# A graph layer and a routed FFN on one core: the graph weight centred over its rows, raw x transposed and multiplied, and the reciprocal deviation applied when the product is split

## The chip, the cores and the metric

The kernel runs on one core of one Trainium2 chip. The metric is the device time of one execution in microseconds (us); lower is better. Five engines work side by side and meet at semaphores: TensorE (PE in the rows, its weight loads PEld), VectorE (DVE), ScalarE (ACT), GpSimd (POOL) and SyncE (SP), which only issues transfers.

## The reference

`x` is 4096 x 256, `adj` a 4096 x 4096 matrix of zeros and ones, both in float32.

```python
deg = jnp.maximum((adj != 0).astype(jnp.float32).sum(-1), 1.0)
x = x + gnn(_layernorm(x), adj, deg[..., None], W, b)
x = x + ffn(_layernorm(x)[None], Wr, br, W1, b1, W2, b2)[0]

def _layernorm(x, axis=-1, eps=1e-05):
    m = jnp.mean(x, axis=axis, keepdims=True)
    v = jnp.var(x, axis=axis, keepdims=True)
    return (x - m) / jnp.sqrt(v + eps)

def gnn(x, adjacency, node_degree, W, b):
    a_hat = adjacency + jnp.eye(n)
    dinv = jax.lax.rsqrt(node_degree)
    pooled = (dinv * a_hat * dinv) @ x + x
    return jax.nn.relu(pooled @ W + b)
```

`ffn` sends each token to two of 16 experts (256 to 512 to 256, GELU between) and adds the weighted results to its input. The change concerns the first layernorm and its product with `W` alone.

## The kernel before, in words

The 4096 rows are 32 tiles of 128 (`T = 32`). The kernel has three stages.

**The first tile.** For each of the 32 row tiles, n = 0 to 31, the product y = layernorm(x) @ W is made and kept in two float16 parts, `yh` and `yl`, whose sum carries more digits than one of them. A tile passes through the engines like this: VectorE takes its statistics (`stats_of`, L797) and, once for a chunk of eight tiles, turns them into mean and variance (`stats`, L803 to L819); GpSimd raises the variance to the power -1/2 and makes the shift (`rstd0`, L1221 and L1224), again for eight tiles in one instruction; ScalarE writes the normalised tile (`normalize`, L703); TensorE transposes it (`x_T`, L499); ScalarE copies the transpose out of PSUM (`copy_x_T`, L710); TensorE multiplies it with W (`x_times_W`, L507); ScalarE writes the high part (`high_y`, L714); VectorE writes the low part (`low_y`, L839). ScalarE runs `normalize(n)`, `copy_x_T(n - 1)`, `high_y(n - 2)` in that order for each n, and each engine takes its instructions strictly in the order of its program.

In the same loop TensorE already works on the first tile of the graph product: at step n it adds the contribution of row tile j = n - 6 (`LAG = 6`; `neighbours`, L484 and L486), which needs `y_low(j)` and, at j = 0, 8, 16 and 24, the adjacency chunk that VectorE has turned (`transpose_chunk`, L832, counted by `at_made`). VectorE's program says where the four chunks are turned: chunk 0 after `low_y(3)`, chunks 1 to 3 at the start of the next group of eight, that is after `low_y(7)`, `low_y(15)` and `low_y(23)`.

**The other 31 tiles** of the graph product follow, 64 float16 products each, then the **expert stage** over 79 blocks of 128 tokens.

x comes in 16 transfers of 256 KB, four to a chunk of eight tiles: chunks 0 and 1 half from SP's queue and half from ACT's, chunks 2 and 3 from SP's. W is one transfer of 256 KB on SP's queue (L349). The adjacency comes from POOL's queue (L252), four transfers to a tile. Names in the rows: `wall` is the large buffer that holds x, the normalised tiles, their transposes and the two parts of y; `orows` holds W; `bank` is a PSUM bank; `abuf` the adjacency as it arrived and `at_xg` as it was turned.

Of the kernel before, what the change touches and what calls it, by code (L numbers as in the profile page):

```python
# [52 lines left out]
XR = 4  # L53
# [31 lines left out]
def build(nc, x, adj, gnn_W, gnn_b, Wr, br, W1, b1, W2, b2, out):  # L85
# [13 lines left out]
    xn = wall[:, 0:2 * XR * D].bitcast(F32).rearrange("p (n d) -> p n d", d=D)  # L99
    xnT = wall[:, 2 * XR * D:2 * (XR + 2) * D].bitcast(F32).rearrange("p (n d) -> p n d", d=D)  # L100
# [49 lines left out]
    mean = sb("mean", [P, T], F32)  # L150
    rstd = sb("rstd", [P, T], F32)
    st6 = sb("st6", [P, XC, XT, 6], F32)
    var8 = sb("var8", [P, XC, XT], F32)
    dif8 = sb("dif8", [P, XT], F32)
    minus = sb("minus", [P, T], F32)
    shift0 = sb("shift0", [P, T], F32)
# [36 lines left out]
    tri = st6.rearrange("p c k s -> p (c k s)").bitcast(F16)[:, 0:E * E].rearrange("p (e f) -> p e f", f=E)  # L193
# [9 lines left out]
    ps_Y = (banks[6], banks[7])  # L203
# [231 lines left out]
    def _(pe):  # L435
# [57 lines left out]

        def x_T(n):
            after(pe, "x_normed", n)
            if n >= 2:
                after(pe, "x_T_copied", n - 2)
            for c in range(DC):
                mm = pe.transpose(ps_xT[n % 2][:, c * P:(c + 1) * P], xn[:, n % XR, c * P:(c + 1) * P], id32[:, :])  # L499
            mm.then_inc(ev("x_T"), 1)  # L500

        def x_times_W(n):
            after(pe, "x_T_copied", n)
            if n >= 2:
                after(pe, "y_low", n - 2)
            for c in range(DC):
                mm = pe.matmul(ps_Y[n % 2][:, 0:D], xnT[:, n % 2, c * P:(c + 1) * P], wg_arrival[:, c, :],  # L507
                               start=c == 0, stop=c == DC - 1)
            mm.then_inc(ev("y_made"), 1)

        def first_tile():

            for n in range(T + LAG):
                if n < T:
                    x_T(n)
                if 0 <= n - 1 < T:
                    x_times_W(n - 1)
                j = n - LAG
                if j >= 0:
# [37 lines left out]
        pe.wait_ge(ev("constants"), CONSTANTS)  # L557
        pe.wait_ge(ev("w_gnn_in"), 16)
        pe.matmul(ps_P[:, 0:E], ones16[:, :], firsts[:, :], start=True, stop=True)
# [87 lines left out]
    def _(act):  # L647
# [50 lines left out]
        def normalize(n):  # L698
            if n % XT == 0:
                after(act, "x_shift", n // XT)  # L700
            if n >= XR:
                after(act, "x_T", n - XR)
            act.activation(xn[:, n % XR, :], xin[:, n, :], ACT.Identity, scale=rstd[:, n:n + 1], bias=shift0[:, n:n + 1])\  # L703
               .then_inc(ev("x_normed"), 1)

        def copy_x_T(n):
# [3 lines left out]
            act.activation(xnT[:, n % 2, :], ps_xT[n % 2][:, 0:D], ACT.Copy).then_inc(ev("x_T_copied"), 1)  # L710
# [9 lines left out]
        for n in range(T + 2):  # L720
            if n < T:
                normalize(n)
            if 0 <= n - 1 < T:
                copy_x_T(n - 1)
            if 0 <= n - 2 < T:
                high_y(n - 2)
            if n == 2:
# [62 lines left out]
    def _(dve):  # L790
# [3 lines left out]
        def stats_of(c, k):  # L794
            if k == 0:
                V.wait_ge(x_in[c], 16 * Q)
            V.bn_stats(st6[:, c, k, :], xin[:, c * XT + k, :]).then_inc(ev("bn"), 1)  # L797

        def stats(c):
            after(V, "bn", c * XT + XT - 1)  # L800
            m_e, m_o = st6[:, c, :, 1], st6[:, c, :, 4]
            v_e, v_o = st6[:, c, :, 2], st6[:, c, :, 5]
            V.tensor_tensor(mean[:, c * XT:(c + 1) * XT], m_e, m_o, ALU.add).then_inc(ev("mean_sum"), 1)  # L803
            V.tensor_tensor(dif8[:, :], m_e, m_o, ALU.subtract).then_inc(ev("dif"), 1)
            V.tensor_tensor(var8[:, c, :], v_e, v_o, ALU.add).then_inc(ev("var_sum"), 1)
            after(V, "mean_sum", c)
            V.tensor_scalar(minus[:, c * XT:(c + 1) * XT], mean[:, c * XT:(c + 1) * XT], -0.5, None, ALU.mult)\
             .then_inc(ev("minus_made"), 1)
            after(V, "minus_made", c)
            after(V, "dif", c)  # L810
            V.tensor_tensor(dif8[:, :], dif8[:, :], dif8[:, :], ALU.mult).then_inc(ev("dif2"), 1)

            after(V, "dif2", c)
            after(V, "var_sum", c)
            V.scalar_tensor_tensor(out=var8[:, c, :], in0=dif8[:, :], scalar=D / 4.0, in1=var8[:, c, :],
                                   op0=ALU.mult, op1=ALU.add).then_inc(ev("var_made"), 1)
            after(V, "var_made", c)

            V.tensor_scalar(var8[:, c, :], var8[:, c, :], 1.0 / D, EPS, ALU.mult, ALU.add)\  # L819
             .then_inc(ev("var_ready"), 1)  # L820

# [517 lines left out]
```

## Time and profile before

| | before |
|---|---|
| median of 3 runs | 668.12 us (667.94 to 670.16) |
| the profiled execution | 667.72 us |
| its span (first to last instruction) | 666.1 us |
| TensorE busy | 598.5 us, 90% of the span |
| VectorE busy | 456.1 us, 68% |
| GpSimd busy | 335.6 us, 50% |
| ScalarE busy | 231.9 us, 35% |
| granted TensorE clock, mean | 0.977 |

The span leaves 1.6 us of the execution outside it. A row's line numbers are those of the kernel before. The rows that the prediction uses stand in the section before it.

### The profile page before, as it was taken

The page shows a single profiled execution, that of the slowest core. Times are in us where ns is not written, and L with a number is a line of the kernel's source. Part 1 is how long each engine was busy: PE and PEld are TensorE (multiplying, and loading weights), DVE is VectorE, ACT ScalarE, POOL GpSimd, SP SyncE. Part 2 cuts the span into 40 slices and gives each one's busy share as a digit, 9 for nine tenths or more (in the row PEclk, how much of TensorE's full clock was granted, in tenths as well). Part 3 has the DMA queues.
Part 4 walks back from the last instruction along what each step waited for, and adds up shares of the span by engine and source line. Part 5 has one row for each costly group of instructions (what it writes and reads, how often), then busy time and mean ns, then how long its engine had stood idle before and what let it go on. Part 6 is the DMA issues. An engine that isn't in the chain of part 4 may idle for free. (4 is left out here: it accounts for less than half of the span.)

```text
span 666.1 us, 17021 instructions
## 1 busy us (share of the span) xinstructions
PE 598.5 (90%) x4796; PEld 462.3 (69%) x4797; DVE 456.1 (68%) x1369; ACT 231.9 (35%) x483; POOL 335.6 (50%) x375
## 2 busy tenths in 40 slices
PE   2999999999999999999943999899999999999993
PEld 1687888888888788888831666566666777676772
DVE  2665888888888788888873666577665565565562
ACT  2785333332333222333330444343433323332331
POOL 6232466667666667766451123455444444434443
PEclk9999999999999999999975999999999999999998
DMA  8908699999999989999287344566654443343420
GB/s 228 236 13 160 132 195 196 196 193 190 190 196 180 196 171 190 193 198 200 87 316 242 99 113 110 127 141 138 136 84 75 80 80 67 67 75 64 74 49 1
DMA packets 67450, 94.60 MB, mean 142 GB/s; under 512 B 9232, under 2 KB 42288, under 8 KB 66896
## 3 DMA queue, kind: packets, MB, share of 16 engines
q0 software_dynamic: 32928, 51.03, 45.4%
q1 hardware_dynamic: 32176, 40.32, 19.7%
q10 hardware_dynamic: 2304, 2.72, 1.2%
q8 instruction: 22, 0.36, 0.2%
q14 instruction: 20, 0.16, 0.1%
HBM read 103.71 MB, written 25.83 MB: 194 GB/s over the span
## 5 line engine op out<-in xcount | busy, mean ns | idle before, releaser
L484 PE MATMUL bank<-wall,at_xg 128*128 128x257 f16 x1024 | 238.6, 274 | 5.9 <-DVE at_xg L832 5.8
L486 PE MATMUL bank<-wall,at_xg 128*128 128x256 f16 x1024 | 233.1, 273 | 0.0
L1299 POOL DMA_INDIRECT out_dram<-orows,at_xg x79 | 128.1, 1622 | 179.2 <-DMA out_dram<-orows,at_xg 98.0
L590 PE MATMUL bank<-wall,feat 128*128 (+1 forms) x474 | 117.2, 384 | 10.9 <-issue 7.9
L484 PEld LDWEIGHTS bank<-wall,at_xg 128*128 128x128 f16 x1024 | 102.8, 100 | 28.0 <-DVE at_xg L832 13.9
L769 ACT ACTIVATE hgs<-hgs 128x512 f32<-128x512 f32 x79 | 49.8, 630 | 198.2 <-DVE hgs L1123 195.9
L1129 DVE SCALAR_TENSOR_TENSOR hl<-bank,xseT 128x512 f16<-128x512 f32 x79 | 54.6, 692 | 92.1 <-ACT xseT L775 68.5
L1269 POOL DMA_INDIRECT rows<-feat,posi x64 | 66.7, 1042 | 91.1 <-issue 91.1
L486 PEld LDWEIGHTS bank<-wall,at_xg 128*128 128x128 f16 x1024 | 100.3, 98 | 15.0
L613 PE MATMUL bank<-wall,xseT 128*128 (+1 forms) x632 | 108.1, 273 | 0.0
L590 PEld LDWEIGHTS bank<-wall,feat 128*128 128x128 f16 x474 | 45.9, 98 | 59.1 <-issue 23.8
L832 DVE STREAM_TRANSPOSE at_xg<-abuf 128x512 int32<-128x512 int32 x128 | 86.6, 696 | 0.4
L613 PE MATMUL bank<-wall,hl 128*128 (+1 forms) x316 | 86.1, 273 | 0.0
L252 POOL DMA_DIRECT2D abuf<-in_adj_dram x128 | 72.8, 588 | 3.7 <-DVE at_xg L832 1.5
L613 PEld LDWEIGHTS bank<-wall,xseT 128*128 128x128 f16 x632 | 61.8, 98 | 8.2
L1123 DVE SCALAR_TENSOR_TENSOR hgs<-bank,abuf 128x512 f32<-128x512 f32 x79 | 53.8, 681 | 0.1
L1112 DVE COPY feat<-bank 128x512 f16<-128x512 f16 x79 | 33.3, 422 | 23.7 <-PE bank L568 21.4
L598 PE MATMUL bank<-id,hgs 128*128 128x128 f32 x316 | 47.9, 274 | 0.0
L775 ACT ACTIVATE xseT<-bank 128x512 f16<-128x512 f32 x79 | 45.7, 578 | 0.3 <-PE bank L598 0.3
L690 ACT ACTIVATE orows<-orows,bs 128x256 f32<-128x256 f32 x32 | 19.2, 600 | 76.2 <-DVE bs L918 76.2
L568 PEld LDWEIGHTS bank<-id,at_xg 128*128 128x128 f16 x316 | 24.2, 99 | 27.1 <-issue 5.7
L1137 DVE TENSOR_SCALAR orows<-bank,at_xg 128x256 f32<-128x256 f32 x79 | 37.6, 475 | 2.3 <-PE bank L613 2.3
(146 smaller groups left out, 802.2 us busy)
## 6 DMA issues: line engine op xcount, KB each, us to landing
abuf<-in_adj_dram POOLq DMA_DIRECT2D x128, 256.0 KB
wst<-in_L_ffn_W_dram SPq DMA_DIRECT2D x32, 512.0 KB
at_xg<-rows SPq DMA_DIRECT2D x79, 136.0 KB
out_dram<-orows SPq DMA_DIRECT2D x32, 128.0 KB
abuf<-in_L_ffn_b_dram SPq DMA_DIRECT2D x4, 1024.0 KB
wall<-in_x_dram SPq DMA_DIRECT2D x12, 256.0 KB, 13.9
rows<-pad ACTq DMA_DIRECT2D x12, 136.0 KB, 2.7
out_dram<-orows,at_xg POOLq DMA_INDIRECT x79
```

The lines of the kernel that those rows point to most:

```text
L252: eng.dma_start(arrived[b * PQ:(b + 1) * PQ, k % AB, :, :], adj_v[bass.ds(pair(i, k), 1), k % 2, b, :, :, :].rearrange("n i a c -> i (n a) ...
L484: both = [lambda: pe.matmul(ps_acc[odd][:, 0:D + 1], w, yh[:, j, 0:D + 1], start=j == 0, stop=j == T - 1), lambda: pe.matmul(ps_acc[odd][: ...
L486: lambda: pe.matmul(ps_acc[odd][:, 0:D], w, yl[:, j, :], start=False, stop=False)]
L590: mm = pe.matmul(q_h[r % 2][:, :], a, w, start=n == 0, stop=n == 3 * DC - 1)
L598: mm = pe.transpose(q_g[r % 2][:, c * P:(c + 1) * P], hg[r % 2][:, c * P:(c + 1) * P], id32[:, :])
L613: mm = pe.matmul(q_o[r % 2][:, 0:D], a, w, start=False, stop=n == 3 * HC - 1)
L769: act.activation(hg[r % 2], hg[r % 2], ACT.Gelu).then_inc(ev("gelued"), 1)
L832: V.transpose(at[:, c, :].bitcast(I32).rearrange("p (n a i) -> p a n i", a=Q, i=PQ), arrived[:, k % AB, :, c * CW // CH:(c + 1) * CW // CH ...
L1123: V.scalar_tensor_tensor(out=hg[r % 2], in0=q_h[r % 2][:, :], scalar=1.0 / (SX * SW), in1=b1all[:, bass.ds(e * H, H)], op0=ALU.mult, op1=A ...
L1129: V.scalar_tensor_tensor(out=hl[:, r % 2, :], in0=q_g[r % 2][:, :], scalar=SH, in1=hh[:, r % 2, :], op0=ALU.mult, op1=ALU.subtract).then_i ...
L1269: L.indirect_dma_start(rows, at_place, feat[:, odd, k, :], None).then_inc(listed[odd], 16)
L1299: L.indirect_dma_start(out, bass.IndirectOffsetOnAxis(ap=info[r][:, 0:1].bitcast(U32), axis=0), orow[r], None, bounds_check=N - 1, oob_is_ ...
```

## The change

The mean of a row need not be taken out of x: if the mean over its rows is taken out of each column of W, a constant added to a row of x adds nothing to the product. So the change

- makes W's column means with two products against a matrix of 1/256 (`column_means`) and subtracts them from W (`centre_W`, two VectorE instructions);
- transposes x itself as it arrived; `normalize`, the means, `minus` and `shift0` are gone;
- takes the variance in nine groups of 2, 3, 3 and six times 4 tiles in place of four of 8, five VectorE instructions and one GpSimd instruction each, in place of seven and two;
- multiplies by the reciprocal deviation (with the scale of the high part in it) when the product is split: `high_y` becomes an Identity with a scale that is a column of `rstd`, and `low_y` takes the same column as its scalar;
- gives the product three PSUM banks in place of two;
- takes the statistics of tile n + 5 after `low_y(n)` (`LEAD = 5`), and turns the four adjacency chunks after `low_y(4)`, `low_y(12)`, `low_y(20)` and `low_y(28)`;
- puts W first in SP's queue, and GpSimd makes the identity matrix and the exponents before its first adjacency loads; the loads of the adjacency's second and third tile stand behind the fourth and the sixth `rstd0`.

```diff
+GROUPS = ((0, 2), (2, 5), (5, 8)) + tuple((n, n + 4) for n in range(8, 32, 4))
+LEAD = 5
...
+        sp.dma_start(wg_arrival, gnn_W.rearrange("(c p) n -> p c n", p=P)).then_inc(ev("w_gnn_in"), 16)
         for b in QUEUE[0]:
             load_x(sp, 0, b)
-        sp.dma_start(wg_arrival, gnn_W.rearrange("(c p) n -> p c n", p=P)).then_inc(ev("w_gnn_in"), 16)
...
+            for c in range(DC):
+                mm = pe.matmul(ps_mean[:, 0:D], one_dth, wg_arrival[:, c, :], start=c == 0, stop=c == DC - 1)
+            mm.then_inc(ev("w_means"), 1)
...
         def x_T(n):
-            after(pe, "x_normed", n)
+            if n % XT == 0:
+                pe.wait_ge(x_in[n // XT], 16 * Q)
...
         def x_times_W(n):
             after(pe, "x_T_copied", n)
-            if n >= 2:
-                after(pe, "y_low", n - 2)
+            if n >= 3:
+                after(pe, "y_low", n - 3)
...
         def high_y(n):
+            for g, (first, _) in enumerate(GROUPS):
+                if n == first:
+                    after(act, "rstd_made", g)
             after(act, "y_made", n)
-            act.activation(yh[:, n, 0:D], ps_Y[n % 2][:, 0:D], ACT.Copy, scale=SY).then_inc(ev("y_high"), 1)
+            act.activation(yh[:, n, 0:D], ps_Y[n % 3][:, 0:D], ACT.Identity, scale=rstd[:, n:n + 1]).then_inc(ev("y_high"), 1)
...
-        for n in range(T + 2):
+        for n in range(T + 1):
             if n < T:
-                normalize(n)
+                copy_x_T(n)
             if 0 <= n - 1 < T:
-                copy_x_T(n - 1)
-            if 0 <= n - 2 < T:
-                high_y(n - 2)
...
+                high_y(n - 1)
...
+        def variance(g):
+
+            first, end = GROUPS[g]
+            cols = slice(first, end)
+            after(V, "bn", end - 1)
+            V.tensor_tensor(dif[:, cols], st6[:, cols, 1], st6[:, cols, 4], ALU.subtract).then_inc(ev("dif"), 1)
+            V.tensor_tensor(var[:, cols], st6[:, cols, 2], st6[:, cols, 5], ALU.add).then_inc(ev("var_sum"), 1)
...
+        centre_W()
+        for n in range(LEAD):
+            stats_up_to(n)
+        for n in range(T):
+            low_y(n)
+            if n + LEAD < T:
+                stats_up_to(n + LEAD)
+            if n % XT == XT // 2:
+                transpose_chunk(0, 0, n // XT)
...
+        for g in range(len(GROUPS)):
+            rstd0(g)
+            if g in (3, 5):
+                for b in range(Q):
+                    load_adj(L, 0, (g - 1) // 2, b)
```

TensorE's program at its start, before the change. L499 is a transposition, L507 the product with W, and the brackets say what an instruction waits for.

```order
L559 MATMUL bank<-firsts,ones 128x16 [waits w_gnn_in,constants]
L499 MATMUL bank<-id,wall 128x128 [waits x_normed]
L499 MATMUL bank<-id,wall 128x128
L499 MATMUL bank<-id,wall 128x128 [waits x_normed]
L499 MATMUL bank<-id,wall 128x128
L507 MATMUL bank<-orows,wall 128x256 [waits x_T_copied]
```

And with the change, where L498 is the product for the column means, L507 the transposition and L515 the product with W.

```order
L498 MATMUL bank<-orows,wall 128x256 [waits one_dth,w_gnn_in]
L498 MATMUL bank<-orows,wall 128x256
L507 MATMUL bank<-id,wall 128x128 [waits x_in0,p_id32]
L507 MATMUL bank<-id,wall 128x128 x3
L515 MATMUL bank<-orows,wall 128x256 [waits x_T_copied,w_centred]
L515 MATMUL bank<-orows,wall 128x256
```

The transposition no longer waits for a normalised tile but for x's first chunk, and the first product waits for the centred W.

VectorE's program around the turning of the adjacency's third chunk (L832, STREAM_TRANSPOSE), before the change: it stands right behind `low_y(15)` (L839), ahead of the statistics (L797) for tiles 24 and on.

```order
L803 TENSOR_TENSOR mean<-st 128x8 [waits bn]
L804 TENSOR_TENSOR dif<-st 128x8
L805 TENSOR_TENSOR var<-st 128x8
L807 TENSOR_SCALAR minus<-mean 128x8 [waits mean_sum]
L811 TENSOR_TENSOR dif<-dif 128x8 [waits dif,minus_made]
L815 SCALAR_TENSOR_TENSOR var<-dif,var 128x8 [waits var_sum,dif2]
L819 TENSOR_SCALAR var<-var 128x8 [waits var_made]
L839 SCALAR_TENSOR_TENSOR wall<-bank,wall 128x256 [waits y_high] x4
L832 STREAM_TRANSPOSE at_xg<-abuf 128x4x4x32 [waits a_in0]
```

With the change the second chunk is turned (L838) behind `low_y(12)` (L845) and `stats_of(17)` (L808); the rows begin with the variance of group 12 to 15, which `high_y(12)` waits for.

```order
L815 TENSOR_TENSOR dif<-st 128x4 [waits bn]
L816 TENSOR_TENSOR var<-st 128x4
L818 TENSOR_TENSOR dif<-dif 128x4 [waits dif]
L820 TENSOR_SCALAR var<-var 128x4 [waits var_sum]
L824 SCALAR_TENSOR_TENSOR var<-dif,var 128x4 [waits var_eps,dif2]
L865 SCALAR_TENSOR_TENSOR gbm<-orows,gbm 64x256 [waits gb_high]
L845 SCALAR_TENSOR_TENSOR wall<-bank,rstd,wall 128x256 [waits y_high]
L808 BN_STATS st<-wall 128x6 [waits x_in2]
L845 SCALAR_TENSOR_TENSOR wall<-bank,rstd,wall 128x256 [waits y_high]
L808 BN_STATS st<-wall 128x6
L838 STREAM_TRANSPOSE at_xg<-abuf 128x4x4x32 [waits a_in0]
```

The chunk that `neighbours(8)` needs was turned behind `low_y(7)` before, and is turned behind `low_y(12)` now; the chunks for `neighbours(16)` and `neighbours(24)` move from `low_y(15)` and `low_y(23)` to `low_y(20)` and `low_y(28)`.

## Rows read from the trace of the kernel before

**Rows 1.** The page's costliest groups: busy us, mean ns, idle time before it.

```profile
L832 DVE STREAM_TRANSPOSE at_xg<-abuf 128x512 int32<-128x512 int32 x128 | 86.6, 696 | 0.4
```

**Rows 2.** Windows: stretch, its length, busy us (count) by engine, PEclk, DMA share, GB/s.

```profile
64.00:341.00 277.00, 266.73 (x2380) 225.24 (x2378) 231.12 (x880) 85.92 (x201) 176.38 (x229) 1.00 0.87 183
```

**Rows 3.** Who waited for whom in the first 80 us: total, times, longest.

```profile
ACT wall L703 <- POOL shift L1224: 11.8, 4, 8.5
PE bank L559 <- DMA orows<-in_L_gnn_W_dram: 11.8, 1, 11.8
PE bank L499 <- ACT wall L703: 3.1, 4, 1.4
```

**Rows 4.** Timeline of TensorE: start, length, what, count, idle before it.

```profile
13.29 1.18 PE L499 MATMUL bank<-id,wall 128*128 128x128 f32 x4 [1.37 <-ACT wall L703]
14.45 2.07 PE L507 MATMUL bank<-orows,wall 128*128 128x256 f32 x4
...
16.75 1.71 PE L507 MATMUL bank<-orows,wall 128*128 128x256 f32 x4
...
18.86 0.44 PE L499 MATMUL bank<-id,wall 128*128 128x128 f32 x2 [0.40 <-ACT wall L703]
...
20.31 1.03 PE L507 MATMUL bank<-orows,wall 128*128 128x256 f32 x4
...
23.55 0.27 PE L484 MATMUL bank<-wall,at_xg 128*128 128x257 f16 x1
...
26.46 0.44 PE L499 MATMUL bank<-id,wall 128*128 128x128 f32 x2 [0.92 <-ACT wall L703]
...
50.75 1.03 PE L507 MATMUL bank<-orows,wall 128*128 128x256 f32 x4
...
52.06 1.03 PE L507 MATMUL bank<-orows,wall 128*128 128x256 f32 x4
52.92 0.27 PE L484 MATMUL bank<-wall,at_xg 128*128 128x257 f16 x1
...
63.26 0.28 PE L484 MATMUL bank<-wall,at_xg 128*128 128x257 f16 x1 [1.23 <-DVE at_xg L832]
```

**Rows 5.** Timeline of ScalarE: a scaled Identity, a Copy from SBUF, one from PSUM.

```profile
17.90 0.42 ACT L729 ACTIVATE gbm<-orows 128x256 f16<-128x256 f32 x1 [0.96 <-DMA brb<-in_L_ffn_br_dram]
18.22 0.58 ACT L703 ACTIVATE wall<-wall,shift,rstd 128x256 f32<-128x256 f32 x1
...
51.82 0.38 ACT L714 ACTIVATE wall<-bank 128x256 f16<-128x256 f32 x1 [0.16 <-PE bank L507]
```

**Rows 6.** Timeline of VectorE.

```profile
6.78 2.71 DVE L797 BATCH_NORM_STATS2 st<-wall 128x6 f32<-128x256 f32 x8 [5.35 <-DMA wall<-in_x_dram]
...
16.00 0.75 DVE L797 BATCH_NORM_STATS2 st<-wall 128x6 f32<-128x256 f32 x2 [5.44 <-DMA wall<-in_x_dram]
...
52.23 0.43 DVE L839 SCALAR_TENSOR_TENSOR wall<-bank,wall 128x256 f16<-128x256 f32 x1 [0.26 <-ACT wall L714]
...
61.15 0.42 DVE L839 SCALAR_TENSOR_TENSOR wall<-bank,wall 128x256 f16<-128x256 f32 x1 [0.66 <-ACT wall L714]
...
62.50 1.29 DVE L832 STREAM_TRANSPOSE at_xg<-abuf 128x512 int32<-128x512 int32 x2
...
72.59 0.48 DVE L877 SCALAR_TENSOR_TENSOR pooled<-bank,deg,xseT 128x256 f32<-128x256 f32 x1
```

**Rows 7.** GpSimd's two powers: of 8 columns (timeline), of 1 (the tile's row: ns, min/median/max).

```profile
10.64 1.68 POOL L1221 TENSOR_TENSOR rstd<-var,mhalf 128x8 f32<-128x8 f32 x1 [1.52 <-DVE var L819]
...
L1252 POOL TENSOR_TENSOR vr<-vr,mhalf x32: 566/612/627, 66.2 to 341.3; 128x1 f32<-128x1 f32 x32
```

**Rows 8.** DMA queues (q1 SP, q10 ACT, q0 POOL) from 7 to 12 us: packets, MB.

```profile
q0 software_dynamic: 306, 0.56, 60.4%
q1 hardware_dynamic: 300, 0.37, 24.6%
q10 hardware_dynamic: 242, 0.43, 23.3%
```

More of the change, by code:

```diff
@@ L202, in build @@
     ps_xT = (banks[4], banks[1])
-    ps_Y = (banks[6], banks[7])
+    ps_Y = (banks[6], banks[7], banks[3])
+    ps_mean = banks[5]
     q_x = [b[:, :].bitcast(F16) for b in banks[0:2]]
@@ L515, in first_tile @@
                     x_T(n)
+                if n == 1:
+                    after(pe, "w_centred", 0)
                 if 0 <= n - 1 < T:
@@ L555, in step @@
                     logits(s)
[L557 to L559 removed]
+        column_means()
+        pe.wait_ge(ev("p_id32"), 2)
         first_tile()
@@ L696, in exps @@
             act.activation(ex2[:, :], p8[:, 0:1], ACT.Exp, scale=-1.0, bias=p8[:, 1:2]).then_inc(ev("exps_made"), 1)
[L698 to L704, printed above, removed]
         def copy_x_T(n):
@@ L791, in _ @@
         V = dve
[L794 to L820, printed above, removed]
@@ new lines, in centre_W, with stats_of @@
+        def centre_W():
+            after(V, "w_means", 0)
+            for c in range(DC):
+                mm = V.tensor_tensor(wg_arrival[:, c, :], wg_arrival[:, c, :], ps_mean[:, 0:D], ALU.subtract)
+            mm.then_inc(ev("w_centred"), 1)
+        def stats_of(n):
+            if n % XT == 0:
+                V.wait_ge(x_in[n // XT], 16 * Q)
+            V.bn_stats(st6[:, n, :], xin[:, n, :]).then_inc(ev("bn"), 1)
+        def variance(g):
[4 more added lines that the diff above has]
+            V.tensor_tensor(var[:, cols], st6[:, cols, 2], st6[:, cols, 5], ALU.add).then_inc(ev("var_sum"), 1)
+            after(V, "dif", g)
+            V.tensor_tensor(dif[:, cols], dif[:, cols], dif[:, cols], ALU.mult).then_inc(ev("dif2"), 1)
+            after(V, "var_sum", g)
+            V.tensor_scalar(var[:, cols], var[:, cols], 1.0 / D / SY ** 2, EPS / SY ** 2, ALU.mult, ALU.add)\
+             .then_inc(ev("var_eps"), 1)
+            after(V, "dif2", g)
+            after(V, "var_eps", g)
+            V.scalar_tensor_tensor(out=var[:, cols], in0=dif[:, cols], scalar=0.25 / SY ** 2, in1=var[:, cols],
+                                   op0=ALU.mult, op1=ALU.add).then_inc(ev("var_ready"), 1)
@@ L838, in low_y, with stats_up_to @@
             after(V, "y_high", n)
-            V.scalar_tensor_tensor(out=yl[:, n, :], in0=ps_Y[n % 2][:, 0:D], scalar=SY, in1=yh[:, n, 0:D],
+            V.scalar_tensor_tensor(out=yl[:, n, :], in0=ps_Y[n % 3][:, 0:D], scalar=rstd[:, n:n + 1], in1=yh[:, n, 0:D],
                                    op0=ALU.mult, op1=ALU.subtract).then_inc(ev("y_low"), 1)
-        for k in range(XT):
-            stats_of(0, k)
-        stats(0)
-        for c in range(XC):
-            if c > 0:
-                transpose_chunk(0, 0, c)
-            for k in range(XT):
-                if c + 1 < XC and k < XT // 2:
-                    stats_of(c + 1, 2 * k)
-                    stats_of(c + 1, 2 * k + 1)
-                if c + 1 < XC and k == XT // 2:
-                    stats(c + 1)
-                low_y(c * XT + k)
-                if c == 0 and k == 3:
-                    transpose_chunk(0, 0, 0)
-            if c == 0:
+        def stats_up_to(n):
+            stats_of(n)
+            for g, (_, end) in enumerate(GROUPS):
+                if n == end - 1:
+                    variance(g)
+        centre_W()
[7 more added lines that the diff above has]
+                transpose_chunk(0, 0, n // XT)
+            if n == T // 4 + 2:
                 after(V, "gb_high", 0)
@@ L1169, in _ @@
         L = pool
-        for b in range(Q):
-            load_adj(L, 0, 0, b)
-        L.memset(ones16[:, :], 1.0).then_inc(ev("p_ones16"), 1)
         L.memset(id32[:, :], 0.0).then_inc(ev("p_id32"), 1)
```

60 lines of the change are left out of this document (28 added, 32 removed).

## The prediction

> **What bounds the kernel now.** I read the windows first. From 64 to 341 us TensorE is busy 266.7 of 277 us [rows 2], so the 31 later tiles run at TensorE's pace, and the adjacency is no hindrance: in 128 transpositions VectorE sat idle 0.4 us in all ahead of them [rows 1]. The change touches nothing there, nor in the expert stage. What it can move is the point at which the first tile is done. I take as that point the start of `low_y(31)`, 61.15 [rows 6]: the next tile's adjacency is turned at 62.50 [rows 6], after a few small VectorE instructions that the change leaves alone, and everything later hangs on it.
>
> The first tile has three parts in the timeline of TensorE [rows 4]:
> - Up to 13.29 it does next to nothing. x's first chunk is there at 6.78, when VectorE begins its statistics [rows 6], but the power comes at 10.64 [rows 7], and the waits name ScalarE waiting 11.8 us on GpSimd's shift, and TensorE 11.8 us for W [rows 3].
> - From 13.29 to 23.55, where `neighbours(0)` starts. Its first products take 1.71 us for four records (16.75), later ones 1.03 (20.31) [rows 4]. That is the lower of the clock's two levels, 1.2 GHz, against 2.4. The change of pace lies between the row at 16.75 and that at 18.86, where two transpositions' worth of records take 0.44 against 1.18 for twice as many at 13.29. Four records are one `x_times_W`.
> - From 23.55 on with `neighbours`. Two products start at 50.75 and 52.06, so a step takes 1.31 us, and TensorE is full. In between it pauses for `normalize`, as for 0.92 us at 26.46; such waits are 3.1 us in 4, with 1.37 at the very start and 0.40 at 18.86 among them [rows 3, 4].
>
> **The part from `neighbours(0)` to `low_y(31)`, if nothing waited.** 25 steps of 1.305 are 32.6 us, the own rows and the bias product 0.55 (five products at the 0.11 of a float16 product: 52.92 less 52.06 is 0.86 for four records of twice that each), one `neighbours` 0.2, and from the last product's start to `low_y` 1.48 (50.75 to 52.23) [rows 4, 6]. Sum 34.9 us. Before, it took 61.15 - 23.55 = 37.6 [rows 4, 6], so 2.7 were pauses. Of these 1.3 are waits for `normalize` (3.1 less 1.37 and 0.40), which the change removes with their cause; 1.4 are scattered short ones whose cause I don't know, and which I keep.
>
> **The start, step by step.** (1) *W first.* Chunk 0 waits behind 0.26 MB more. From 7 to 12 us the three queues moved 0.56 + 0.37 + 0.43 = 1.36 MB, 0.27 MB per us [rows 8]. If only the bytes count, chunk 0 comes 1.0 us later, 7.8. If its last SP quarter takes over the place in which W stood, it comes when W came, 11.6 (the waits say 11.8 with the engine's own start) [rows 3]. The turns go by packets (306, 300 and 242), and W's are smaller, which is why W was slow in a crowd and should be quick in front, before the adjacency joins. I take 8.2, near the first end. W itself is there some 3 us earlier, and its means (two products at the lower clock, 1.7 us) and the two subtractions (0.8, as two `low_y`) are done by about 8.2; they are hidden by x's arrival, and would cost up to their 2.5 us if x came first. (2) *Normalisation leaves the path.* `x_T(0)` starts at 8.2 in place of 13.29, and the first product 1.16 later, as before (14.45 less 13.29) [rows 4]: 9.4. The reciprocal deviation is needed only by `high_y(0)`, after that product (11.3): two statistics 0.7, five small VectorE instructions some 0.75, a power of two columns 0.76. The last I get from 0.61 for one column and 1.68 for eight [rows 7], 0.15 a column. That is 10.4, hidden with 0.9 to spare, and if it weren't hidden it would delay `high_y(0)` alone. (3) *The clock.* Before, TensorE worked from 13.29, and the pace changed between 16.75 and 18.86 [rows 4], 3.5 to 5.6 us later. I take 4.8 after 8.2, that is 13.0. At the lower level a step takes 2.2 us (14.45 to 16.75 is 2.3), at the upper 1.1 (1.31 less 0.22 for `neighbours`) [rows 4]. Products start at 9.4, 11.6, 13.7, 14.8 and 15.9, the last being n = 4; the pair of PSUM banks no longer matters, since `y_low(0)` is done by 12.3.
>
> "TensorE: Matmul & The Clock Gate" of the Trainium skill (Part 1) says that the point at which the matmuls become fast differs between runs of one kernel. No row here shows two runs. By it the 13.0 could as well be 1 us earlier or later; a us more at the lower level costs half a us of work.
>
> (4) *`neighbours(0)`* waits for chunk 0 of the adjacency, now turned after `low_y(4)` and a statistic. From product 4's start: `high_y` 1.07 later (50.75 to 51.82); its length now 0.47 for 0.38, so `low_y` starts at 1.57. What a scale from a column costs I take from ScalarE: Identity with two columns 0.58, plain Copy from SBUF 0.42 [rows 5], 0.08 to 0.09 each. Ends: nothing (the copy), or 0.2 (the Identity). `low_y` with a column 0.48 (the row at 72.59) [rows 6] less 0.08 of overlap, the statistic 0.34 (2.71 over 8), then the turning: 0.76 from its start to TensorE's (62.50 to 63.26) [rows 4, 6]. Sum 3.07, near 1 us after TensorE would be ready. So `neighbours(0)` starts at about 18.7, in place of 23.55. The adjacency is no hindrance: 1.05 MB at 0.56 per 5 us [rows 8] are 9.4 us, so it lands by 16.4 even if it only began at 7; a few small GpSimd instructions now ahead of it are under a us, and it is wanted at 17.9. x's chunk 1, 16.00 before [rows 6], is wanted at 16.8.
>
> **What the change adds after that.** At `neighbours(8)`, (16) and (24) the same 3.07 stands against 52.92 - 50.75 = 2.17 [rows 4], at which TensorE is ready: product 12, 20 or 28 starts, 2.17 later the next chunk's `neighbours` is due, and the chunk is there at 3.07. **A stall of 0.90.** Before, it had been turned five steps earlier. On top, 12, 20 and 28 are first tiles of a group. The group's last statistic (15) stands after `low_y(10)`, which starts at -2.61 + 1.57 = -1.04 counted from product 12. `low_y` 0.40, statistic 0.34, variance 0.74, power of four columns 1.06: 1.50, against 1.07. **0.45 more**, since `high_y`, `low_y` and the turning all stand behind it. Sum 1.35, 1.35, and 1.0 for the last (no statistic left): 3.7 us. With the two ends for the Identity 3.1 to 4.7. ScalarE itself falls from three instructions a step to two, and TensorE's work is the same but for the two products; the fourth adjacency load is issued a few us later against the work, and it has two tiles of 8.9 us (277 over 31) of cover.
>
> **Sum.** 18.7 + 34.9 + 3.7 + 1.4 = 58.7, against 61.15: **2.4 us earlier.** Carried to the end one for one, the profiled 667.72 becomes 665.3; against the median, 668.12, it is 665.7. A measurement of this kernel tells some 0.5%, 3.3 us, from no change.
>
> **The rivals.**
> - *The chunk stalls don't come* (VectorE's and ScalarE's latencies overlap better than the sum says, or the pauses hide in the 1.4). For it: ScalarE has a third less to do, and the stages need not add up as they stand. Against it: the order is fixed and each term has a row. It gives back 3.7: 6.1 faster, 662.0.
> - *x's first chunk comes late.* Three transfers in line on SP's queue, taken by turns with ACT's and POOL's: chunk 0 at 11.6 in place of 8.2. Everything up to `neighbours(0)` is 3.4 later: 1.0 slower than before, 669.1, and if the clock rises late too, 670. It decides from 10.6 on (8.2 + 2.4). Against it, W was slow when three queues were busy, and now goes ahead of the third. "DMA: Bandwidth & Descriptors" of the Trainium skill (Queues, rings and completion order) says that each DMA engine takes the queues in turn, packet by packet; by that, W's many small packets in front of x on one queue hold x back, which speaks for this rival, and the near-equal packet counts agree [rows 8].
> - *The gain is lost later*: the 31 tiles or the expert stage wait for something that doesn't move with TensorE, and the time stays at 668. For it, the 1.4 us of unknown pauses and a DMA share of 0.87 [rows 2]; against it, VectorE's 0.4 us [rows 1].
>
> **How the numbers follow.** Forecast 0.58, its own range 664.0 to 667.4 from the ends of chunk 0's arrival, clock and Identity (0.7 to 4.2 faster); a quarter of it is over 3.3 us. No stalls 0.18, all over. Late x 0.12, a third of it slower by over 3.3. Lost later 0.12. Faster: 0.15 + 0.18, and 0.02 for both luck in the clock and few stalls, 0.35. Slower: 0.04, and 0.03 for late x with late clock, 0.07. Same 0.58. The range takes in most of the two outer cases: 661.7 to 669.2.
>
> **What would show it.** `x_T(0)` near 8.2; the fast products from about 13; `neighbours(0)` at 18.7; TensorE's idle rows ahead of L483 "<-DVE at_xg L838", four, three of them of 1 to 1.4 us; the Identity at 0.47; the powers of four columns at 1.06; `low_y(31)` at 58.7, and from there to the end as long as before. I am wrong if chunk 0 lands after 10, if L483's waits are short, or if `low_y(31)` moves and the end doesn't.

## The result, and the profile after

The changed kernel takes 670.85 us (median of 20 runs, 665.5 to 673.78) against 668.77 (20 runs of the kernel before, 666.71 to 670.4): ratio 1.0031, 95% interval 1.0018 to 1.0043. It is 2.1 us slower where 2.4 faster was forecast, and above the whole forecast range, 664.0 to 667.4. A ratio here or below need not be the quotient of the two medians beside it. The profiled execution took 669.26 us, its span 667.6.

The first tile did almost exactly what was predicted. TensorE's timeline of the changed kernel shows it (L498 the column means, L507 the transpositions, L515 the products with W, L483 `neighbours`):

```profile
5.42 2.07 PE L498 MATMUL bank<-orows,wall 128*128 128x256 f32 x4 [5.42 <-DMA orows<-in_L_gnn_W_dram]
8.86 1.09 PE L507 MATMUL bank<-id,wall 128*128 128x128 f32 x4 [1.37 <-DMA wall<-in_x_dram]
10.09 2.05 PE L515 MATMUL bank<-orows,wall 128*128 128x256 f32 x4
...
13.97 1.03 PE L515 MATMUL bank<-orows,wall 128*128 128x256 f32 x4
...
19.28 0.29 PE L483 MATMUL bank<-wall,at_xg 128*128 128x257 f16 x1 [1.02 <-DVE at_xg L838]
...
31.46 0.28 PE L483 MATMUL bank<-wall,at_xg 128*128 128x257 f16 x1 [1.57 <-DVE at_xg L838]
...
43.96 0.28 PE L483 MATMUL bank<-wall,at_xg 128*128 128x257 f16 x1 [1.34 <-DVE at_xg L838]
...
55.57 0.28 PE L483 MATMUL bank<-wall,at_xg 128*128 128x257 f16 x1 [0.99 <-DVE at_xg L838]
```

Against [rows 4], the first transposition is at 8.86 in place of 13.29, the products are at the fast pace (1.03) from 13.97, and `neighbours(0)` is at 19.28 in place of 23.55. The three later rows are the chunk stalls. And `low_y(31)` (L845), which was at 61.15 [rows 6], in VectorE's timeline:

```profile
58.68 0.48 DVE L845 SCALAR_TENSOR_TENSOR wall<-bank,rstd,wall 128x256 f16<-128x256 f32 x1 [0.60 <-ACT wall L721]
...
60.09 1.29 DVE L838 STREAM_TRANSPOSE at_xg<-abuf 128x512 int32<-128x512 int32 x2
...
70.47 1.23 DVE L911 SCALAR_TENSOR_TENSOR wall<-wst,wall 128x1024 f16<-128x1024 f32 x1 [3.74 <-ACT wall L664]
```

So 2.4 us are won at 60.09 (62.50 before, [rows 6]). The last of these rows is where they go: VectorE sits idle 3.74 us at 70.47 until ScalarE's L664 is done. It waited for the same step before too, but 1.79 us:

```profile
70.95 1.23 DVE L905 SCALAR_TENSOR_TENSOR wall<-wst,wall 128x1024 f16<-128x1024 f32 x1 [1.79 <-ACT wall L652]
```

So of the 2.4 us, 0.5 are left here (70.47 against 70.95). VectorE's next adjacency is turned behind it, and TensorE then waits for that, which it didn't at this tile before:

```profile
74.74 0.29 PE L483 MATMUL bank<-wall,at_xg 128*128 128x257 f16 x1 [1.34 <-DVE at_xg L838]
```

ScalarE's L664 makes the high part of the first expert weights in the middle of the second tile. In the timeline of ScalarE after,

```profile
69.38 1.06 ACT L664 ACTIVATE wall<-wst 128x1024 f16<-128x1024 f32 x1 [1.82 <-DMA wst<-in_L_ffn_W_dram]
```

and the same instruction (L652) before, with no wait for a transfer:

```profile
69.87 1.05 ACT L652 ACTIVATE wall<-wst 128x1024 f16<-128x1024 f32 x1
```

The weights' transfer is issued by SP right after the first tile: at 62.62 before, at 60.21 after (timelines of SP, before and after):

```profile
62.62 0.57 SPq L384 DMA_DIRECT2D wst<-in_L_ffn_W_dram  x1
```

```profile
60.21 0.57 SPq L383 DMA_DIRECT2D wst<-in_L_ffn_W_dram  x1
```

It is issued 2.4 us earlier and yet takes 9.1 us to land, at 69.36. The view of its line, over this transfer and the next one, says:

```profile
DMA to landing us min/median/max: 9.1/10.5/11.8
```

What it meets there shows in windows of 4 us, in the columns of [rows 2]. Before:

```profile
54.00:58.00 4.00, 4.00 (x26) 3.36 (x25) 1.27 (x3) 3.51 (x10) 0.41 (x1) 1.00 1.13 201
...
62.00:66.00 4.00, 2.77 (x26) 2.42 (x26) 3.53 (x13) 0.38 (x1) 0.00 (x0) 1.00 0.75 193
66.00:70.00 4.00, 4.00 (x38) 3.54 (x37) 3.11 (x8) 1.01 (x3) 2.30 (x5) 1.00 0.13 19
```

After:

```profile
54.00:58.00 4.00, 3.01 (x18) 2.19 (x17) 1.88 (x4) 1.95 (x5) 3.92 (x8) 1.00 0.42 67
58.00:62.00 4.00, 2.77 (x24) 1.99 (x23) 3.15 (x12) 1.04 (x3) 1.62 (x4) 1.00 1.07 187
62.00:66.00 4.00, 4.00 (x39) 3.51 (x37) 3.71 (x11) 0.99 (x2) 0.72 (x2) 1.00 1.06 205
66.00:70.00 4.00, 4.00 (x39) 3.61 (x37) 0.73 (x2) 1.00 (x2) 2.03 (x4) 1.00 1.11 249
```

Before, the DMA share falls to 0.13 at 66: the weights had landed (at 66.8 in the trace, 4.2 us after their issue) and little else was under way. After, it is low at 54 (0.42) and full from 58 on. The reason is GpSimd's program. Before, the loads of the adjacency's fourth and fifth tile (L252) went out at 49.93 and 52.27; after, the eight loads (L251) stand together behind the last power (timeline of GpSimd after):

```profile
52.85 1.01 POOL L1227 TENSOR_TENSOR rstd<-var,mhalf 128x4 f32<-128x4 f32 x1 [4.21 <-DVE var L824]
...
55.31 4.31 POOL L251 DMA_DIRECT2D abuf<-in_adj_dram  x8
```

The first four of the eight are the fourth tile's adjacency, of which the prediction said that two tiles of cover lie over it. They do, and no transposition waited for it. But its bytes, and those of the fifth tile behind it, pass while the weights pass.

### The profile page after: what moved, and what is told of

It reads as the page before. It is cut to its first block and busy times, and to the rows that moved or that the text cites. A ratio compares the mean times of both kernels' runs of the same rounds, so it can differ in the third digit from the quotient of the medians.

```text
span 667.6 us, 16995 instructions
## 1 busy us (share of the span) xinstructions
PE 599.6 (90%) x4800; PEld 463.0 (69%) x4801; DVE 460.0 (69%) x1389; ACT 220.6 (33%) x451; POOL 335.2 (50%) x376
## 5 line engine op out<-in xcount | busy, mean ns | idle before, releaser
L483 PE MATMUL bank<-wall,at_xg 128*128 128x257 f16 x1024 | 238.7, 274 | 12.4 <-DVE at_xg L838 12.2
L483 PEld LDWEIGHTS bank<-wall,at_xg 128*128 128x128 f16 x1024 | 102.8, 100 | 36.0 <-DVE at_xg L838 22.1
L838 DVE STREAM_TRANSPOSE at_xg<-abuf 128x512 int32<-128x512 int32 x128 | 86.5, 695 | 0.4
L251 POOL DMA_DIRECT2D abuf<-in_adj_dram x128 | 72.7, 584 | 2.9 <-DVE at_xg L838 1.5
L580 PE MATMUL bank<-id,at_xg 128*128 128x128 f16 x316 | 31.0, 221 | 10.4 <-DMA at_xg<-rows 10.4
```

The costliest lines, as they stand in the source:

```text
L251: eng.dma_start(arrived[b * PQ:(b + 1) * PQ, k % AB, :, :], adj_v[bass.ds(pair(i, k), 1), k % 2, b, :, :, :].rearrange("n i a c -> i (n a) ...
L483: both = [lambda: pe.matmul(ps_acc[odd][:, 0:D + 1], w, yh[:, j, 0:D + 1], start=j == 0, stop=j == T - 1), lambda: pe.matmul(ps_acc[odd][: ...
L580: mm = pe.transpose(q_x[r % 2][:, c * P:(c + 1) * P], xg16[r][:, c * P:(c + 1) * P], id16[:, :])
L838: V.transpose(at[:, c, :].bitcast(I32).rearrange("p (n a i) -> p a n i", a=Q, i=PQ), arrived[:, k % AB, :, c * CW // CH:(c + 1) * CW // CH ...
```

## The experiments

Each kernel was run in five rounds beside the kernel before; the tables give the points in the profile. "Tile k" is the start of the pooled sum of tile k (the last VectorE step before its layernorm), "experts" the time from tile 31 to the end of the span. A kernel's *lead* at a point is by how much it is there earlier than the first profile of the kernel before. Each row of points is one profile. Kernels of one table ran together.

| first table | median us | ratio (95%) | `low_y(31)` | tile 2 | tile 31 | experts |
|---|---|---|---|---|---|---|
| before (31 runs; its profile is the first one) | 668.55 | | 61.15 | 80.51 | 339.25 | 326.9 |
| changed, first profile | | | 58.68 | 79.61 | 338.91 | 328.7 |
| `after_again`: changed, unedited | 671.71 | 1.0044 (1.0026, 1.0063) | 59.33 | 82.65 | 340.83 | 329.9 |
| `adj3_early` | 668.23 | 0.9981 (0.9956, 1.0006) | 59.32 | 78.74 | 337.74 | 326.0 |
| `turn_early` | 666.92 | 0.9969 (0.9949, 0.9989) | 54.95 | 79.00 | 337.15 | 328.5 |
| `turn_adj3` | 664.36 | 0.9933 (0.9908, 0.9958) | 54.93 | 74.34 | 333.38 | 329.6 |

**The changed kernel, unedited**, for a second profile. 

> The changed kernel once more, unedited, for a second profile. In the first profile low_y(31) started at 58.68 us (61.15 before), but two tiles later the lead was 0.5 us, and the expert stage took 2 us more than before. Theory A (timing): the lead goes because the expert weights' first transfer now shares the queues with eight adjacency loads; it must show again, low_y(31) at 58.7 +- 0.4 and a lead of 0 to 1 us from the third tile on. For the expert stage, theory B (something fixed in the changed program, such as where its buffers lie, makes it slower) expects the time from the last tile's pooled sum to the end to be 328.5 or more again, against 326.9 before; theory C (its chain of accumulating transfers varies from run to run) expects it anywhere between 326 and 331.

It was worse than in its first profile: VectorE waited 4.51 us for L664, ScalarE 2.59 for the weights, and a stretch at the lower clock was added (last section). A lead of 1.8 at `low_y(31)` became 2.1 us behind at tile 2, more than theory A had allowed for.

**The fourth load behind the eighth power**, so that its bytes pass before the weights:

```diff
-            if g in (3, 5):
+            if g in (3, 5, 7):
...
-            if is_(t, lambda t: t + AB - 1 < T):
+            if is_(t, lambda t: 1 <= t and t + AB - 1 < T):
```

> The changed kernel with one edit: GpSimd issues the adjacency loads of the fourth tile behind the eighth rstd0, inside the first tile, and no longer after the last one. Theory A (the lead of 2.4 us is lost since these loads and the next four meet the expert weights' transfer) expects the weights to land before ScalarE wants them (its wait of 1.8 us and VectorE's of 3.7 gone), the lead at the third tile 2.0 to 2.4 us in place of 0.5, and the time about 2 us below the unedited changed kernel. The rival, that the lead is lost to something else at the second tile (VectorE's own order, the write of the base rows), expects the lead still about 0.5 us at the third tile and the same time.

ScalarE again has no wait for the weights (its timeline):

```profile
68.10 1.05 ACT L664 ACTIVATE wall<-wst 128x1024 f16<-128x1024 f32 x1
```

The weights land 5.6 us after their issue. The lead of 1.83 at `low_y(31)` is 1.77 at tile 2: nothing is lost there now. At tile 31 this kernel is 3.1 us ahead of the unedited one, and its median is 3.5 lower. So the place of that load is what lost the lead. Whether this kernel is faster than the one before its interval doesn't decide.

**The chunks turned earlier**, which undoes the other half of the new order (chunks 1 to 3 are turned where they were before):

```diff
-            if n % XT == XT // 2:
-                transpose_chunk(0, 0, n // XT)
+            if n == XT // 2:
+                transpose_chunk(0, 0, 0)
+            if n % XT == XT - 1 and n < T - 1:
+                transpose_chunk(0, 0, n // XT + 1)
```

> The changed kernel with one edit: adjacency chunks 1 to 3 of the first tile are turned after low_y(7), low_y(15) and low_y(23), as before the change, chunk 0 stays. The sum in the prediction put the stalls at neighbours(8), (16) and (24) at 3.7 us together, so low_y(31) should start at 55.0 to 55.6 in place of 58.7. If the stalls are latency that would sit elsewhere anyway (the group powers alone), low_y(31) comes at 57 or later. Theory A expects that little of it reaches the end while the adjacency loads of the fourth tile stay where they are: a lead at the third tile of 1 us or less and a total within 1 us of the unedited changed kernel; the rival that the lead is carried expects 3 us less.

The stalls at `neighbours(8)`, (16) and (24) are gone, and `low_y(31)` is 4.4 earlier than in `after_again`. The loss behind it stays: by tile 2 only 1.5 of a lead of 6.2 are left. The weights take 10.6 us to land, and TensorE waits 2.84 us for the chain behind them, where the unedited kernel of the same table had 2.11:

```profile
72.52 0.34 PE L483 MATMUL bank<-wall,at_xg 128*128 128x257 f16 x1 [2.84 <-DVE at_xg L838]
```

The loss between the two points is 4.7 us here and 4.0 there. So against the unedited kernel 3.7 of the 4.4 are kept at tiles 2 and 31, and the median is 4.8 lower. Theory A, which wanted it within 1 us, is wrong on that; its rival's 3 us came nearer.

**Both**: 

> Both edits: chunks 1 to 3 turned earlier, and the fourth tile's adjacency loads issued inside the first tile. Theory A expects the gains to add and to be carried: low_y(31) at about 55.3, a lead over the kernel before of 5 to 6 us at the third tile, and a total 5 to 6 us below the unedited changed kernel, that is 2.5 to 4 us below the kernel before if the expert stage still costs 2. The rival (the tiles wait for transfers whatever the first tile does) expects the lead at the third tile to stay below 3 us.

The lead of 6.2 at `low_y(31)` is 6.2 at tile 2 and 5.9 at tile 31. The two defects nearly add up: against the unedited kernel the one edit gives 3.5 us in the median, the other 4.8, both 7.4.

| second table | median us | ratio (95%) | `low_y(31)` | tile 2 | tile 31 | experts |
|---|---|---|---|---|---|---|
| before (29 runs) | 668.86 | | | | | |
| `weights_first` | 670.54 | 1.0018 (0.9993, 1.0043) | 58.34 | 77.76 | 336.53 | 330.6 |
| `before_w_first` | 668.47 | 0.9994 (0.9976, 1.0012) | 60.57 | 79.93 | 338.63 | 328.1 |
| `w_old_place` | 672.74 | 1.0048 (1.0021, 1.0076) | 60.88 | 82.89 | 341.97 | 329.7 |
| `turn_adj3_w` | 663.20 | 0.9912 (0.9879, 0.9945) | 54.66 | 74.07 | 333.00 | 325.5 |

**The weights taken out of the way instead of the load**: the first expert weights issued right after x, at 13.51, into the buffer that is free then.

```diff
+        sp.dma_start(staged(0, 0), w_dram(0, 0)).then_inc(w_in[0], 16)
...
-            if k % 2 == 0 and is_(t, lambda t: t < T):
+            if k % 2 == 0 and is_(t, lambda t: 0 < t < T):
```

> The changed kernel with one edit: the first expert weights' transfer (512 KB into a buffer that is free from the start) is issued by SP right behind x's loads and no longer behind the first tile. The adjacency loads stay as late as the change put them. Theory A (the second and third tile wait for this transfer, which shares the queues with the late adjacency loads, and TensorE's clock falls in the pause) expects ScalarE's wait for it gone, the lead at the third tile 2.0 to 2.5 us, no stretch at the lower clock near 76 us, and a time 3 to 4 us below the unedited changed kernel, as with the adjacency loads moved. The rival, that the late adjacency loads hurt by themselves, expects the lead still under 1 us.

No wait for the weights, and the lead of 2.8 at `low_y(31)` is 2.75 at tile 2 and 2.7 at tile 31. That the two transfers hinder each other is thereby shown from the other side. But the median did not follow, and the expert stage, whose program is the same, was 3.7 longer than in the first profile of before.

**The same edit on the kernel before**: 

> The kernel before with that same edit alone. Theory A says that the kernel before was not waiting for these weights (they landed by 66.8 us, ScalarE took them at 69.9 after its copy of a transpose), so the edit is worth under 0.5 us here, and the time is that of the kernel before. The rival, that an early weight transfer helps by itself whatever the change does, expects 2 us or more here too.

No change, as there was no wait to remove.

**W back behind x's first chunk on SP's queue**, the rest of the change left: 

> The changed kernel with W back in its old place in SP's queue, behind two of the quarters of x's first chunk. The prediction's first term says W first costs x's first chunk 1 to 2 us and saves W 5. If so, x's chunk is there at about 6.8 to 7.2 here, W at 10.5 to 11.6, the first product with the centred W starts at about 14.0 to 14.7 in place of 10.1, and low_y(31) starts 3 to 4.5 us later than with W first, at 62 to 63, later than in the kernel before (61.15). If the change's gain came from the raw transposes alone and W's place didn't matter, low_y(31) stays within 1 us of 58.7 to 59.3.

`neighbours(0)` moves from 19.28 to 21.50 and `low_y(31)` from 58.68 to 60.88: W in front is worth 2.2 us, less than the 3 to 4.5 expected, and without it the change gains 0.3 in the first tile. The first product starts 2.7 later (12.81), but at the fast pace from the second one on. The weights meet the same loads: they take 10.2 us to land, ScalarE waits 2.90 for them, and 0.3 ahead at `low_y(31)` becomes 2.4 behind at tile 2. In the median it was 3.9 slower than before.

**All three edits** (`turn_adj3_w`): 

> All three edits on the changed kernel: chunks 1 to 3 turned earlier, the fourth tile's adjacency loads inside the first tile, the first expert weights behind x. Theory A expects nothing much on top of the two edits without this one, since their lead of 6 us at the third tile was already carried: low_y(31) near 54.9, the same time within 1 us, about 664.4. If the weights' transfer still held something up there, 1 to 2 us less.

It is the fastest, 5.9 us below before by its ratio.

**What happens in the expert stage?** The third group asked for addresses (72 unused floats put the later tensors back where they were), for chance, and for the group's wait.

| third table | median us | ratio (95%) | `low_y(31)` | tile 2 | tile 31 | experts |
|---|---|---|---|---|---|---|
| before (35 runs) | 669.03 | | | | | |
| `before_again` | 668.56 | 0.9986 (0.9971, 1.0002) | 61.30 | 80.66 | 339.40 | 327.2 |
| `wf_again` | 668.93 | 0.9992 (0.9971, 1.0012) | 59.06 | 78.48 | 337.25 | 328.3 |
| `wf_pad` | 668.81 | 0.9987 (0.9971, 1.0003) | 58.62 | 78.03 | 336.68 | 332.3 |
| `wf_lead7` | 668.98 | 0.9983 (0.9961, 1.0006) | 59.01 | 78.43 | 337.15 | 329.9 |

> The kernel before, unedited, as a measure of what a ratio between two equal kernels does. Both theories: ratio 1.000 within 0.2%. The first tile ends (low_y(31)) at 61.2, the last pooled sum at 339.3. The expert stage, from the last pooled sum to the end, was 326.9 in the profile of before. If its length is chance from one execution to the next (theory C), this profile gives anything from 325.5 to 330.6. If the kernel before has a shorter expert stage by a fixed cause (theory B), it is 327 within 0.5.

> The changed kernel with the first expert weights in front of the second tile's adjacency, a second time, as the neighbour of the padded one. Theory B: 2 us slower than the padded kernel. Theory C: the same within 0.2%, and its profile's expert stage, 330.6 the first time, comes out anywhere from 325.5 to 330.6. The last pooled sum at 336.5, as the first time.

> The changed kernel with the first expert weights in front of the second tile's adjacency, and 72 unused floats per partition behind dif, so that every later tensor in SBUF stands at the address that it has before the change (the change takes 288 bytes per partition away). Theory B (the expert stage is longer in the changed kernel because its tensors stand at other addresses): the expert stage is back at 327 and the median 2 us below the same kernel without the 72 floats, near 666.0 against 668.8 of the kernel before. Theory C (chance, or something that has no address in it): no change from the kernel without the floats, both between 667 and 670.5, and the expert stage anywhere from 325.5 to 330.6.

```diff
     dif = sb("dif", [P, T], F32)
+    unused = sb("unused", [P, 72], F32)
```

Addresses are out: the padded kernel has the median of its neighbour and the longest expert stage of all. The same kernel gave 330.6 and 328.3 in two profiles, so much of a profile's stage is chance. An unedited kernel before came out at 0.9986 of itself, which is how finely such ratios can be read.

`LEAD = 7` in place of 5: 

> The same kernel with the statistics seven tiles ahead of low_y in place of five (LEAD = 7). My theory of the first tile: the wait for the group's power (0.45 at tiles 12, 20 and 28) goes, the wait for the chunk (0.9 each) stays, and two more statistics ahead of low_y(0) cost at most 0.7 at the start: low_y(31) at 57.0 to 58.0 against 58.3, and the last pooled sum 0.3 to 1.3 earlier, at 335.2 to 336.2. The rival, that the three waits are of the chunk alone: low_y(31) at 58.3 to 59.0, no gain. In the median at most 1.3 of 668.

ScalarE's waits for the power behind `neighbours(0)` fell from 6.5 us in six to none, and the last chunk stall from 0.99 to 0.46: the group's wait of 0.45 was real there (0.53). At the other two the stall stayed (1.55 and 1.55 against 1.57 and 1.33), because with seven tiles of lead a `variance` stands right ahead of the turning. The start cost 0.7 more (TensorE waits 1.70 at `neighbours(0)`), so nothing came of it: I had expected `low_y(31)` at 57 to 58, and the 59.01 is the rival's number.

**Does the expert stage depend on when it is entered?** The transposition of the last row tile is made seven times over:

```diff
-            for c in range(DC):
+            for c in tuple(range(DC)) * (7 if n == T - 1 else 1):
```

| fourth table | median us | ratio (95%) | `low_y(31)` | tile 2 | tile 31 | experts |
|---|---|---|---|---|---|---|
| before (10 runs) | 669.20 | | | | | |
| `wf_delay` | 671.18 | 1.0041 (1.0027, 1.0054) | 59.12 | 78.54 | 337.32 | 331.2 |
| `before_delay` | 670.96 | 1.0028 (1.0014, 1.0041) | 62.15 | 81.51 | 340.21 | 330.3 |
| `best_again` (`turn_adj3_w` again) | 663.27 | 0.9916 (0.9902, 0.9929) | 53.34 | 72.76 | 331.70 | 330.0 |

> The changed kernel with the first expert weights in front, and the transposition of the last row tile made seven times over (12 transpositions more, 0.22 us each by the 0.44 of a pair: 2.6 us more TensorE work late in the first tile). Expected by both theories: low_y(31) 2.6 later than the 58.3 to 59.1 of the same kernel without it, near 61.3, and the last pooled sum near 339.4, where the kernel before has it. Theory C (the expert stage varies by chance, whatever the start): the median 2.6 above the kernel without the delay, near 671.4. Theory P (the expert stage depends on when it is entered, and has something in it that does not move with the tiles): the delay costs next to nothing, the stage is back at 327, and the median stays at 668.5 to 669.5.

> The kernel before with the same 12 transpositions more. low_y(31) near 63.8, the last pooled sum near 342. Theory C: the median 2.6 above the kernel before, 671.5. Theory P: less than 1.5 above it.

> The changed kernel with all three edits (chunks turned four steps earlier, the fourth adjacency load behind the eighth power, the first expert weights in front), a second time. The last pooled sum at 333.0, as the first time. Theory C: the expert stage anywhere from 325.5 to 332, and a median within 1.5 of the 663.2 of the first time. Theory P: the expert stage at 325.5 within 0.5 again.

The twelve transpositions took 0.11 us each and not 0.22, so the delay was 1.3 us, half of what I wrote. It cost 1.8 in the kernel before. In the changed kernel it cost 1.5 to 3.9 (1.0041 against 0.9983 to 1.0018 without it). No version got it for nothing, which speaks against theory P, and `best_again` speaks against it too: its stage took 330.0 where P wanted 325.5 again. And the kernel before had a long stage (330.3) here too.

Where the stage's length differs can be read. The longer stages wait longer for gathered tokens, nearly all of it in blocks 12 to 18 of the 79: TensorE's longest such wait there is 2.2 us in the first profile of before (414 to 441 us, 2.2 in all) and 2.4 in `wf_pad` (414 to 444, 5.8 in all). The gather itself isn't slow: that of block 14 (counted from 0) takes 2.0 to 2.2 us from issue to landing in all 17 profiles. It is issued late: block 13's goes out 64.5 to 65.4 us behind tile 31 in the five shortest stages and 66.9 to 69.5 in the others. By the program SP issues the gather of block k once the accumulating transfer (the one that adds a block's results to the output) of block k - 8 has landed, and the accumulating transfers wait for each other.

Two of them come out in two lengths, and the lengths go with how soon behind them SP issues the next 512 KB of late expert weights. I read them from the 17 traces, from issue to landing:

| | weights issued behind it | it takes | profiles |
|---|---|---|---|
| third accumulating transfer | 1.34 us or more | 3.8 to 4.0 us | 9: all four of the kernel before, five of changed kernels |
| the same | 1.17 or less | 6.0 to 6.8 | 8, all of changed kernels |
| sixth | 1.32 or more | 2.7 | 5, with the five shortest stages (325.5 to 328.1) |
| the same | 1.20 or less | 4.0 to 5.1 | 12, with the twelve longest |

The thirteen profiles of changed kernels have stages of 325.5 to 332.3, mean 329.2, the four of the kernel before and its edits 326.9 to 330.3, mean 328.1. Behind that stands a difference without overlap: the second accumulating transfer takes 3.2 to 3.3 us in the four and 3.5 to 4.4 in the thirteen, and the weights come 1.9 to 2.0 us behind the third in the four and 0.8 to 1.7 in the thirteen. The changed kernels thus come into this stretch with less margin. Why their second transfer is longer isn't shown, and no run moved the weights there, so that they lengthen the third and the sixth is read from what goes together, and not tested.

## Why the prediction was wrong

- **W first, x's first chunk at 8.2**: near, 8.75 on VectorE and 8.86 on TensorE; over the profiles with W in front `x_T(0)` started between 8.56 and 9.15. The rival that x comes late didn't come. W in front is worth 2.2 us by `w_old_place`. Its means and subtractions (5.42 to 8.28) were hidden as said.
- **Normalisation off the path, first product 9.4**: 10.09, 0.7 later, nearly all of it from x. The power of two columns took 0.73 for 0.76, that of four 1.01 for 1.06.
- **Clock at 13.0**: 13.4 in this profile; over the profiles with W in front 11.9 to 14.9, and `neighbours(0)` lay between 18.37 and 19.97. "TensorE: Matmul & The Clock Gate" of the Trainium skill (Part 1) says that the point at which the matmuls become fast differs between runs of one kernel; these runs agree (13.4 and 14.9 in two profiles of the changed kernel).
- **`neighbours(0)` at 18.7**: 19.28. Half of that miss is a slip in the sum: product 4 at 15.9 and the 3.07 behind it give 19.0, and the whole would then have been 2.1 us faster. The 3.07 itself was good: product 4 started at 16.14, 3.14 ahead.
- **The stalls, 1.35, 1.35 and 1.0, 3.7 in all**: 1.57, 1.34 and 0.99, 3.9 in all. The Identity took 0.47 as said. The scattered 1.4 us were not there: without the stalls (`turn_early`) the part from `neighbours(0)` to `low_y(31)` takes 34.98, against the 34.9 worked out for no wait at all.
- **`low_y(31)` at 58.7**: 58.68. That it is so exact is luck: 0.6 late at the start and stalls 0.2 longer, against 1.4 of pauses that weren't there, leave 0.6 that I can't place.
- **"Carried to the end one for one"**: this is the step that failed, and what it rests on is "the fourth adjacency load is issued a few us later against the work, and it has two tiles of cover". The cover was counted for the load's own consumer. Its 1 MB went out at 55.31 in place of 49.93, with the fifth tile's right behind it, and the weights 2.4 us earlier: they met, the weights landed 9.1 us after their issue in place of 4.2, and VectorE, which is the one that turns the next adjacency, waited 3.74 behind ScalarE in place of 1.79. At tile 31 the lead was 0.34 in one profile, and 1.6 us negative in the other. Moving either transfer away (`adj3_early`, `weights_first`) brings the lead to tile 31, 1.5 of 1.8 and 2.7 of 2.8. In the medians, the unedited kernel stands at 1.0031 and 1.0044, the four kernels with the weights in front between 0.9983 and 1.0018, mean 0.9995: some 2.8 us of the 4.5 between forecast and result.
- **The rival "the gain is lost later"** was the right one, with 0.12, and I put it at no change. It spoke of the 31 tiles waiting for something that doesn't move with TensorE; the weights' landing moved the wrong way, from 66.8, 3 us before ScalarE wanted them, to 69.36, when it was already waiting.
- **What stays open.** With the weights in front 2.0 to 2.7 us of lead reach tile 31, and the mean ratio of 0.9995 says that 0.3 reach the end. The missing 2 us are in the expert stage, which the prediction took as untouched. Neither addresses nor the moment of entry explains them. `turn_early` and `turn_adj3_w` lose next to nothing there (2.1 of lead and 0.9969; 6.3 and 0.9912), but `turn_adj3` loses 1.4 (5.9 and 0.9933) and `best_again`, the same kernel as `turn_adj3_w`, 1.9 (7.6 and 0.9916). Part of it is chance in any one profile. But the smaller margin ahead of the third accumulating transfer stands in all thirteen profiles of changed kernels and in none of the kernel before, so chance isn't all. What makes the second transfer longer there is open.

## What to carry to other kernels

Ask of a transfer that is moved not only whether its consumer has cover, but which other transfer then passes beside it, and who waits for that one: a load with two tiles of slack cost some 3 us by slowing one that had 3 us of slack. An earlier arrival is a gain only if what is wanted next arrives earlier as well; look a whole stage behind the point won, also at waits that were zero with a few us of margin. And removing a stall ahead of such a wait doesn't cure the wait: with the chunks turned earlier 4.7 of 6.2 us of lead were lost at the second tile, and none once the load was moved too.

## What the runs showed of the hardware

- The granted clock can fall in a stretch that is busy on the whole. In `after_again` TensorE, busy without a break worth naming since 61.5, paused 2.11 us ahead of 76.17, and the clock fell to its lower level from 76.4 to 79.8 (granted 0.79 over 74 to 78 us and 0.78 over 78 to 82). A `neighbours` record takes 0.42 us there for 0.27. In `turn_early` the same came at 72.6 to 76.0 after a pause of 2.84. In the first profile, with a pause of 1.34, it didn't, and in `w_old_place`, with one of 2.42 ahead of 78.03, it didn't either (granted 1.00 throughout): the length of the pause alone doesn't decide. Where it falls, a pause costs more than its length: at half the pace, 3.4 us lose 1.7 us of work.
- Such a stretch of 3.4 us also lies in the expert stage of three profiles (from 431.3 in `after_again`, 430.1 in `before_delay`, 422.9 in `before_w_first`), and some of the scatter of the times goes with the clock in both kernels: of the first 20 executions of the changed kernel the seven with a mean granted clock of 0.978 or more took 669.4 on average, the thirteen below 671.6; of the 31 of the kernel before in the first table, the 15 with 0.977 or more took 667.7, the 16 below 669.7.
- The same 512 KB of weights landed by 66.8, 4.2 us after its issue, when it ran beside the end of the earlier loads, and took 9.1 us beside 2 MB of adjacency (9.9, 10.6 and 10.2 in `after_again`, `turn_early` and `w_old_place`).
- GpSimd's power took 0.73, 0.87 and 1.01 us for 2, 3 and 4 columns, beside 0.61 and 1.68 for 1 and 8 [rows 7]: 0.12 to 0.17 a column on a base of some 0.45 to 0.5.
